# Eight row slots instead of four, and expert addresses read without a run-time bounds check, in the routed experts of a decoder layer

## The reference

```
scores = sigmoid(x @ router_weight.T); choose 4 of 16 experts for each token   # tidx, tw
g = einsum('th,eih->tei', x, gate_w);  u = einsum('th,eih->tei', x, up_w)      # 256 -> 128
h = silu(g) * u
yo = einsum('tei,ehi->teh', h, down_w)                                         # 128 -> 256
routed = sum over the 4 chosen experts of tw * yo
out = layernorm(x + routed + shared experts(x))
```

## Time and profile before

| | us |
|---|---|
| runs: median, lowest, highest of 3 | 2103.99, 2087.8, 2117.69 |
| the profiled execution's own time | 2107.94 |
| its span, first to last instruction | 2106.2 |
| stage of the routed experts, first DMA issue to the end of the span | 1662.2 to 2106.2 |
| first and last store of a pair's result | 1678.84, 2049.15 |

### The profile page before, as it was taken

The page is one execution under the profiler, slowest core; times in us unless marked ns, Lnnn a source line. Parts: engine busy times, 40 slices in busy tenths (PEclk is TensorE's granted clock), DMA queues, the critical chain, the costliest instruction groups (busy, mean ns, idle before and its releaser), DMA issues. The chain is left out here.

```text
span 2106.2 us, 35773 instructions
## 1 busy us (share of the span) xinstructions
PE 1646.2 (78%) x11450; PEld 959.7 (46%) x11450; DVE 1260.9 (60%) x3617; ACT 877.0 (42%) x1414; POOL 640.3 (30%) x853
## 2 busy tenths in 40 slices
PE   7969999997887799999899999573536387877770
PEld 4646676775553233333233333251435266656550
DVE  7954555553998788788788886186665001222333
ACT  5535555552332266566566666311112133333330
POOL 2143332301333311111111112262577202033444
PEclk9989999998997699999899999786768698888885
DMA  5797675652678534533533625774456334445563
GB/s 170 224 185 141 112 121 97 116 142 64 189 251 186 80 51 72 81 52 67 87 52 53 99 94 213 240 235 144 141 189 225 120 101 141 126 142 156 176 193 102
DMA packets 207504, 285.81 MB, mean 136 GB/s; under 512 B 55122, under 2 KB 162322, under 8 KB 200430
## 3 DMA queue, kind: packets, MB, share of 16 engines
q1 hardware_dynamic: 168830, 202.39, 35.9%
q0 software_dynamic: 22560, 66.62, 14.7%
q10 hardware_dynamic: 15952, 14.63, 2.8%
HBM read 154.24 MB, written 128.92 MB: 134 GB/s over the span
## 5 line engine op out<-in xcount | busy, mean ns | idle before, releaser
L1470 ACT ACTIVATE sa_prob<-sa_ps_s 128x1024 f32<-128x1024 f32 (+3 forms) x480 | 376.3, 825 | 281.0 <-PE sa_ps_s L1379 200.6
L1529 DVE CUSTOM_DVE_ANT_0 sa_ps_m<-sa_ps_m,sf_later 128x282 f32<-128x282 f32 (+4 forms) x640 | 278.4, 460 | 53.4 <-PE sa_ps_m L1352 52.0
L1532 DVE TENSOR_REDUCE sa_piece_max<-sa_ps_m 128x1 f32<-128x512 f32 x384 | 259.2, 688 | 43.9 <-PE sa_ps_m L1352 43.4
L1506 POOL TENSOR_SCALAR_AFFINE_SELECT sa_prob<-sa_prob 128x256 f32<-128x256 f32 x256 | 102.2, 406 | 500.5 <-ACT sa_prob L1470 497.9
L1352 PE MATMUL sa_ps_m<-sa_k,sa_q 96*128 96x512 bf16 (+4 forms) x768 | 210.6, 335 | 21.0 <-DVE sa_max_parts L1560 7.4
L2200 DVE TENSOR_TENSOR mo_h<-mo_silu,mo_ps_gu 128x256 f32<-128x256 f32 x72 | 30.3, 421 | 315.3 <-ACT mo_silu L2143 244.6
L2095 PE MATMUL mo_ps_gu<-mh_table,mo_xT 128*128 x576 | 176.0, 460 | 41.5 <-ACT mo_xT L2136 38.8
L2187 POOL DMA_INDIRECT mo_picked<-s_ys,mp_row x128 | 123.9, 968 | 180.5 <-DMA s_ys<-mo_y 141.4
L1352 PEld LDWEIGHTS sa_ps_m<-sa_k,sa_q 96*128 96x128 bf16 x768 | 66.4, 99 | 241.5 <-issue 110.6
L1379 PE MATMUL sa_ps_s<-sa_q,sa_k 99*128 99x512 bf16 (+3 forms) x672 | 160.8, 334 | 2.1 <-ACT sa_prob L1470 2.0
L2095 PEld LDWEIGHTS mo_ps_gu<-mh_table,mo_xT 128*128 128x128 f32 x576 | 125.9, 230 | 69.2 <-issue 50.1
(11 more groups left out here) (289 smaller groups left out, 3159.7 us busy)
## 6 DMA issues: line engine op xcount, KB each, us to landing
s_xs<-sa_zero SPq DMA_DIRECT2D x18, 1024.0 KB, 9.9
mo_rows<-s_xs SPq DMA_DIRECT2D x72, 256.0 KB, 3.0
s_ys<-mo_y SPq DMA_DIRECT2D x72, 256.0 KB, 2.2
la_q<-s_q_parts POOLq DMA_DIRECT2D x72, 128.0 KB, 6.0
la_k<-s_k_parts POOLq DMA_DIRECT2D x72, 128.0 KB, 7.8
sa_q<-s_q_parts SPq DMA_DIRECT2D x72, 128.0 KB, 5.1
sa_k<-s_k_parts SPq DMA_DIRECT2D x66, 128.0 KB, 7.1
s_y<-la_y SPq DMA_DIRECT2D x16, 512.0 KB, 3.6
```

Source lines behind the costliest of these rows:

```text
L1470: nc.scalar.activation(dst, src, ACT.Exp, scale=HD ** -0.5).then_inc(expd[s], 1)
L1506: nc.gpsimd.affine_select(out=square, in_=square, compare_op=ALU.is_ge, fill=0.0, base=0, pattern=[[0, 2], [1, P]], channel_multiplier=-1) ...
L1529: nc.vector.tensor_tensor_reduce(ps_m[:, s, 0:hi - lo], ps_m[:, s, 0:hi - lo], later[:, BANK + lo - first:BANK + hi - first], 1.0, -BIG, A ...
L1532: nc.vector.tensor_reduce(piece_max[:, j, t, n:n + 1], ps_m[:, s, 0:hi - lo], AX.X, ALU.max).then_inc(piece_done[s], 1)
```

## The change

The rows of the pairs get eight buffers (`ROW_SLOTS` = 8) instead of four, with a semaphore each; the results `y` keep four. SP loads eight pairs ahead at the start, and in turn q it issues the load of pair q + 8. The four addresses that PE reads for two pairs are taken without the check at run time that each lies between 0 and the last expert's column. All else stays: the order on every engine, the DMAs' sizes, the arithmetic.

```
-        rows = ph.sb("rows", [P, SLOTS, 2, C])
+        rows = ph.sb("rows", [P, ROW_SLOTS, 2, C])
...
-        rows_in, y_out = ph.sems("rows_in", SLOTS), ph.sems("y_out", SLOTS)
+        rows_in, y_out = ph.sems("rows_in", ROW_SLOTS), ph.sems("y_out", SLOTS)
...
             def load_rows(q):
-                if q >= SLOTS:
-                    sp.wait_ge(x_ps, q - SLOTS + 1)
-                sp.dma_start(rows[:, q % SLOTS], ...).then_inc(rows_in[q % SLOTS], 16)
+                if q >= ROW_SLOTS:
+                    sp.wait_ge(x_ps, q - ROW_SLOTS + 1)
+                sp.dma_start(rows[:, q % ROW_SLOTS], ...).then_inc(rows_in[q % ROW_SLOTS], 16)
...
-            for q in range(SLOTS):
+            for q in range(ROW_SLOTS):
                 load_rows(q)
...
-                if q + SLOTS < PAIRS:
-                    load_rows(q + SLOTS)
+                if q + ROW_SLOTS < PAIRS:
+                    load_rows(q + ROW_SLOTS)
...
-                pe.wait_ge(rows_in[q % SLOTS], (q // SLOTS + 1) * 16)
+                pe.wait_ge(rows_in[q % ROW_SLOTS], (q // ROW_SLOTS + 1) * 16)
...
-                        places.first[0:1, 2 * q:2 * q + LOADED], engines=(mybir.EngineType.PE,), min_val=0, max_val=(EXPERTS - 1) * EXPERT_W)
+                        places.first[0:1, 2 * q:2 * q + LOADED], engines=(mybir.EngineType.PE,),
+                        min_val=0, max_val=(EXPERTS - 1) * EXPERT_W, skip_runtime_bounds_check_because="a block's owner is one of the experts")
```

More of the change, by code:

```diff
@@ L1995, in routed_experts @@
     SLOTS = 4
+    ROW_SLOTS = 8
     LOADED = 4
@@ L2030, in load_rows @@
             def load_rows(q):
-                if q >= SLOTS:
-                    sp.wait_ge(x_ps, q - SLOTS + 1)
-                sp.dma_start(rows[:, q % SLOTS], io["xs"][list_rows(q)].rearrange("(s p) c -> p s c", p=P)).then_inc(rows_in[q % SLOTS], 16)
+                if q >= ROW_SLOTS:
+                    sp.wait_ge(x_ps, q - ROW_SLOTS + 1)
+                sp.dma_start(rows[:, q % ROW_SLOTS], io["xs"][list_rows(q)].rearrange("(s p) c -> p s c", p=P)).then_inc(rows_in[q % ROW_SLOTS], 16)
             def load_acc(n):
@@ L2079, in turn_x @@
                         at = a * COLS + s * P
-                        last = nc.tensor.transpose(ps_x[:, q % 2, at:at + P], rows[:, q % SLOTS, s, a * P:(a + 1) * P], ident[:, :])
+                        last = nc.tensor.transpose(ps_x[:, q % 2, at:at + P], rows[:, q % ROW_SLOTS, s, a * P:(a + 1) * P], ident[:, :])
                 last.then_inc(x_ps, 1)
```

## The result

The changed kernel takes 2002.4 us (median of 4 runs, 2000.3 to 2004.2), the kernel before 2110.8 (4 runs, 2087.8 to 2121.3). The ratio is 0.9521, with a 95% interval of 0.9436 to 0.9605; it is taken from the means without the slowest run of the kernel before, 2121.3, which lies over 1.5% above its fastest. The profiled execution took 2002.49 us, with a span of 2000.8.

What follows compares the result with a forecast made beforehand. Late rows, the exposed address load with its check, and a 0.85 clock bound the last stage. At 3.25 us per pair, then gather-bound roots, the span fell 116 us to 1989.9; forecast 1988, range 1968 to 2030.

Steps and rivals of the forecast that it cites:

- Row wait and address load at nothing: PE in the last stage: waits of 0.82 and 1.17 us per two pairs both go to 0, pair time 3.25 us.
- The cover: SP's row loads: eight slots give 15.2 us of lead from issue to use, against landings of 2.7 to 7.0.
- the 0.66 us of transposes: PE: without the check, the remaining 0.333 us address load fits under the 0.66 us of transposes issued just before.
- the check alone would cost little with eight slots: PE's sequencer: the address check, if left in, was expected to cost little, since the slots do the work.
- The bound of the gathers: POOL and DVE: at 3.25 us per pair gathers become the bound; DVE waits in `combine` for tiles 2, 4 and 5.
- The sum: Last stage, stores and roots added in turn: pair 31 at 1779.6, root 3 at 1870.6, root 5 at 1925.4, end 1989.9.
- The 26.2 us from a first gather to its root: POOL: a tile's root comes 26.2 us after its first gather, used for roots 1 and 3.
- The 3.25 us for a cold pair: PE before root 3: after idling, one pair counted at double time, 3.25 us more.
- The clock rival: PE's clock stays low, late pairs keep a slow gate_up: pair time 4.0, median 2019 us; chance 0.12.
- The exposed load: Rival: PE's address load stays exposed, 1.15 us in every two pairs: 3.83 per pair, median 2011; chance 0.07.
- The gathers' rival: Gathers slow beside rows and stores, 1.48 us apart against 1.26: 25 us over tiles 1 to 7, median 2012; chance 0.10.
- DVE blocks DMA: Rule: two-port DVE instructions keep GpSimd from writing DMA descriptors; four closings among gathers would cost up to 5.6 us.

Runs made afterwards that it cites:

- the first experiment: The changed kernel with eight row slots but the run-time address check put back: 2002.9 us, ratio 0.9542 against the kernel before.
- the 7.3 of the experiment: The changed kernel without the loads of rows after the first eight pairs: 1991.8 us, ratio 0.9482, last stage 7.3 us less than the changed kernel's.

## Why the prediction was right

The forecast was 1988 in a range of 1968 to 2030; measured were 2002.4. Of the 14.4 us, 7.0 are the stage's later start in the profiled execution (1669.5 against 1662.6), which lies ahead of all that the change touches; 3.9 lie in the stage; the rest is most of the 3.95 that I took off because the profiled execution of before lay above its median, while that of after lies on it.

*Row wait and address load at nothing: right.* PE waits for rows only before the first pair and 0.3 us for addresses, and the pair time is 3.25 to the hundredth up to pair 31. The cover was enough: the longest landing is 8.4 us, the lead 15.2. The address load is hidden in another place than the working had it, not under the 0.66 us of transposes: where the check was kept it runs under the gate_up of the pair before, as the first experiment shows. That the check alone would cost little with eight slots was right as well, by the first experiment, and still right with twice the loads.

*The bound of the gathers: right.* DVE stands in `combine` for tiles 2, 4 and 5, the gathers lead the chain, and moving five roots moved the end.

*The sum, step by step, from the first load of rows.* Pair 31's store: 114.8 us after it, 117.1 forecast, since the first pair came 2.2 earlier. That goes with the check: in the three kernels that check four addresses at a time the first store stands 16.1 to 16.8 us after the first load, in the others 14.1 to 15.2, and the sum had kept the old value. Store 31 to root 1: 32.4 against 29.2. Root 1 to 2: 28.3 against 27.4. Root 2 to the store of pair 47: 2.3, as taken between 0 and 3.25. Store 47 to root 3: 32.7 against 32.1. Roots 3 to 5: 56.4 against 54.8. Root 5 to the end: 64.3 against 64.5. Together 331.3 against 327.4. That they lie so close is in part luck: 9.2 us too few for the gathers of tiles 1 to 5 stand against 2.3 too many before pair 31 and 2.9 at root 3, for a cold pair.

*Two terms were mis-sized, and one of them hid the other.* The 26.2 us from a first gather to its root were read where DMA traffic was lower; with pairs at 3.25 us beside them they are 28.6 for tile 1 and 29.7 for tile 3, and 26.1 and 25.8 where the loads are taken away. (For tile 1 the first gather also came 3.85 us after the store in place of 3.0.) I had put this only into a rival, and there as a slower issue of gathers; the issue kept its pace (16 gathers in 20.1 to 20.4 us for tiles 1 to 4), the landing was late. The 3.25 us for a cold pair behind tile 2 were wrong in place: the cold pair came behind the stop for tile 2's first gathers (the gate_up of 3.17 us at 1830.63), ahead of root 2, for which the gathers were waited for anyway. The clock was back before pair 47, and from there to pair 55 the stores are 26.0 us apart, eight times 3.25. Root 3 was set by its gathers, not by the loop.

*The rivals.* The clock rival fell: 1.00 over 120 us of unbroken work. The exposed load fell. The gathers' rival was right that they end later, by 7 to 9 us (the 7.3 of the experiment, and 3.2 + 0.9 + 3.5 + 1.6 over what the sum had for tiles 1 to 5) and not 25, and wrong in the way, since the issue did not slow down. The page "SBUF — State Buffer" of the Trainium skill (the "DVE blocks DMA" trap) stays without support here: the sixteen gathers of tile 2, with a closing of 1.37 us among them, kept to 20.2 us. Whether a closing runs in a two-port mode no row here shows, so its rule is not refuted either.

## What to carry to other kernels

A buffer's depth and the place of its load in the issuing queue are one question: count the time from issue to use, not the slots. Two waits that stand one behind the other in the same place need not both be removed; once the first is gone, the sequencer may run far enough ahead to hide the second. And when a loop gets faster, look for the chain that then ends last, here an in-order queue that stood still between two tiles, and try that next.

## What was not expected of the hardware

With loads, stores and gathers together the DMA engines came to 0.93 of their time at 288 GB/s, and beside the gathers a 256 KB load of rows took 8.4 us to land (five slots), against a median of 3.0 and a longest of 7.0 before. That the loads in turn delay the gathers, the experiment without them shows. Reading two addresses took PE's sequencer longer, 537 ns, than reading four, 332; why stays open.
